# Attention scores in plain float32 on sixteen 32x32 array tiles, with K turned on the host

## The reference

```
scores = einsum('bsgrd,btgd->bgrst', xq, xk) / sqrt(32)     # 8 groups g, 4 heads r, 32 numbers d
scores = scores + mask                                      # s: 32 rows, t: 257 tokens
probs  = softmax(scores);  out = einsum('bgrst,btgd->bsgrd', probs, xv)
```

## Time and profile before

| | |
|---|---|
| median of 2 runs | 1293.69 us (1291.55 to 1295.84) |
| span of the profiled execution | 1290.8 us, 42154 instructions |
| PE busy | 1238.7 us, 96% |
| PEld busy | 1074.4 us, 83% |
| ACT busy | 1122.5 us, 87% |
| DVE busy | 1046.6 us, 81% |
| POOL busy | 824.7 us, 64% |
| DMA | 166.45 MB, 270940 packets, 195433 of them under 512 B |
| chain of work that ended last | PE 86%, DVE 4%, SP's queue 3% |

### The profile page before, as it was taken

One profiled execution on the slowest core, in us unless ns is written; L12 is line 12 of the kernel. 1 busy time (PEld: TensorE's weight loads), 2 busy tenths in 40 slices (PEclk: granted clock), 3 DMA queues, 4 the chain that ended last, 5 costly groups with the idle time before them and its releaser, 6 DMA issues.

```text
span 1290.8 us, 42154 instructions
## 1 busy us (share of the span) xinstructions
PE 1238.7 (96%) x13676; PEld 1074.4 (83%) x13676; DVE 1046.6 (81%) x3552; ACT 1122.5 (87%) x3337; POOL 824.7 (64%) x1259
## 2 busy tenths in 40 slices
PE   4679999999999999999999999999999999999997
PEld 3558888888888888888888888888888888888886
DVE  7978788888888888888888888878888888888753
ACT  5999898998999899899998989998999999898851
POOL 5376666776666677666667766667776666676420
PEclk9899999999999999999999999999999999999999
DMA  8754445554545545454454555445445445554210
GB/s 230 172 133 127 113 128 138 133 143 121 138 127 129 138 123 145 130 140 120 135 138 122 145 131 134 125 121 144 129 123 153 130 116 138 129 140 123 60 59 33
DMA packets 270940, 166.45 MB, mean 129 GB/s; under 512 B 195433, under 2 KB 253298, under 8 KB 270722
## 3 DMA queue, kind: packets, MB, share of 16 engines
q1 hardware_dynamic: 270722, 163.74, 47.5%
HBM read 128.50 MB, written 34.08 MB: 126 GB/s over the span
## 4 chain that ended last, share of the span: by engine, by line
PE 86%; DVE 4%; SPq 3%; issue 2%; DMA 2%; ACT 2%; POOL 1%; DVEq 0%; ACTq 0%; POOLq 0%
PE ps_p L566 25%; PE ps_p L637 16%; PE ps_p L652 15%; PE ps_p L665 14%; PE ps_p L598 9%; PE ps_s L578 8%; SPq L385 2%; DVE ms L1401 1%; DMA dn<-den 1%; ACT pr L853 1%; DVE x L1257 0%; DMA qx<-turn_q 0%; SPq L373 0%; DMA vl<-in_ctx 0%; PE ps_p L524 0%
## 5 line engine op out<-in xcount | busy, mean ns | idle before, releaser
L853 ACT ACTIVATE pr<-ms,negmax 128x256 f32<-128x256 f32 x1024 | 514.7, 505 | 3.8 <-DVE negmax L1401 3.7
L1401 DVE CUSTOM_DVE_ANT_0 ms<-ps_s,neg_mask,last 128x256 f32<-128x256 f32 x1024 | 457.5, 471 | 34.9 <-PE ps_s L578 30.2
L785 ACT ACTIVATE pts<-ps_p 128x512 f32<-128x512 f32 x512 | 295.9, 592 | 48.2 <-PE ps_p L566 44.2
L566 PE MATMUL ps_p<-ident,pr 128*128 128x128 f32 x2048 | 304.8, 277 | 12.0 <-ACT pr L853 4.9
L566 PEld LDWEIGHTS ps_p<-ident,pr 128*128 128x128 f32 x2048 | 238.2, 141 | 49.2 <-issue 16.0
L853 ACT ACTIVATION_READ_ACCUMULATOR pr<-ms,negmax 128x1 f32 x1024 | 200.6, 196 | 0.0
L1075 POOL TENSOR_TENSOR kt<-kr,kt 128x512 fp32r<-128x512 f32 x128 | 165.1, 1290 | 27.9 <-ACT kt L785 27.3
L652 PE MATMUL ps_p<-wa_hi,ut_hi 128*128 128x288 f32 x512 | 177.7, 347 | 1.4 <-DVE ut_lo L1217 1.4
L652 PE MATMUL ps_p<-wa_lo,ut_hi 128*128 128x288 f32 x512 | 151.0, 295 | 0.0
L652 PE MATMUL ps_p<-wa_hi,ut_lo 128*128 128x288 f32 x512 | 150.7, 294 | 0.0
L1117 POOL TENSOR_TENSOR lastp<-lastp 128x256 f32<-128x256 f32 (+4 forms) x320 | 128.7, 402 | 22.6
(11 more groups left out here) (140 smaller groups left out, 2709.6 us busy)
## 6 DMA issues: line engine op xcount, KB each, us to landing
cx<-in_ctx SPq DMA_DIRECT2D x128, 256.0 KB, 3.0
kx<-in_ctx SPq DMA_DIRECT2D x512, 64.0 KB, 2.4
xq<-in_x SPq DMA_DIRECT2D x32, 512.0 KB, 4.2
turn_q<-xq SPq DMA_DIRECT2D x32, 512.0 KB, 3.7
qx<-turn_q SPq DMA_DIRECT2D x128, 128.0 KB, 3.0
xr<-in_x SPq DMA_DIRECT2D x32, 512.0 KB, 4.4
out_x<-tmp SPq DMA_DIRECT2D x32, 512.0 KB, 5.2
dn<-den SPq DMA_DIRECT2D x512, 2.0 KB, 2.0
```

What stands on the lines that cost most here:

```text
L566: mm = pe.transpose(into[:, j * P:(j + 1) * P], source, ident[:, :])
L785: return act.activation(out, in_, ACT.Copy, scale=scale)
L853: act.activation(pr[:, b % 2, g, :], ms[:, n % MS, :], ACT.Exp, bias=negmax[:, n % MS:n % MS + 1], scale=-1.0, accum_out=den[:, b, g:g + 1 ...
L1401: dve.tensor_tensor_reduce(ms[:, n % MS, :], ps_s[:, g % GPH, g // GPH * SW:(g // GPH + 1) * SW], neg_mask[:, 0:SW], 1.0, last[:, it % 2, ...
```

## The change

The host gives K turned (`io["keys"]`: 128 partitions of quad and d, then half and token). SP loads a batch with one DMA of 2 KB rows into `kt`, which is now plain float32. `k_turn`, `k_high`, `k_low`, `q_high` and `q_low` are gone; `q_turn` writes straight into `qr`, which has two buffers. `scores` multiplies plain float32, and takes the four r apart: each matmul has 32 rows, 32 columns of weights and 256 moving columns and stands in one of the 16 places of 32x32, in 2 halves x 4 r x 4 quads = 32 matmuls for each batch. A matmul of plain float32 is again load, pass, load, pass.

```diff
             def load_keys(tile, b):
 
-                if at(tile, BPT, b - 1) > 0:
-                    sp.wait_ge(kr_done, at(tile, BPT, b - 1))
-                turned = context[tile * BPT + b:tile * BPT + b + 1, 0:2 * P, :].rearrange(
-                    "o (c t) (q e) -> (o t) c q e", t=HEAD_DIM, q=GPH)
-                for quad in range(GPH):
-                    sp.dma_start(kx[HEAD_DIM * quad:HEAD_DIM * (quad + 1), b % 2, :, :, :].rearrange("p c h d -> p c (h d)"),
-                                 turned[:, :, quad, :]).then_inc(kx_loaded[b], 16)
+                if tile > 0:
+                    sp.wait_ge(s_done, at(tile - 1, BPT * GPH, GPH * (b + 1)))
+                sp.dma_start(kt[:, b, :, :].rearrange("p h t -> p (h t)"),
+                             io["keys"][tile * BPT + b:tile * BPT + b + 1, :, :].rearrange("o p c -> (o p) c")).then_inc(kx_loaded[b], 16)
...
             def scores(it, b):
-                pe.wait_ge(kl_done, at(it, BPT, b + 1))
+                pe.wait_ge(kx_loaded[b], at(it, 16, 16))
                 if b == 0:
-                    pe.wait_ge(ql_done, at(it, 2, 2))
+                    pe.wait_ge(qr_done, at(it, 2, 2))
                 pe.wait_ge(ms_done, at(it, STEPS, GROUPS * b))
                 for h in range(HALVES):
-                    for j, (q_part, k_part) in enumerate(((0, 0), (0, 1), (1, 0))):
+                    for r in range(REP):
                         for quad in range(GPH):
                             rs = slice(HEAD_DIM * quad, HEAD_DIM * (quad + 1))
-                            mm = pe.matmul(ps_s[:, quad, h * SW:(h + 1) * SW], qs[rs, it % 2, q_part, b, h, :, :].rearrange("p r s -> p (r s)"),
-                                           kt[rs, b, k_part, h, :], start=(j == 0), stop=(j == 2), skip_group_check=True)
-                            if j == 2 and h == HALVES - 1:
+                            mm = pe.matmul(ps_s[SEQ * r:SEQ * (r + 1), quad, h * SW:(h + 1) * SW], qr[rs, it % 2, h, b, r, :],
+                                           kt[rs, b, h, :], start=True, stop=True, skip_group_check=True)
+                            if r == REP - 1 and h == HALVES - 1:
                                 mm.then_inc(s_done, 1)
...
-            def k_turn(tile, b):
-                dve.wait_ge(kx_loaded[b], at(tile, 64, 64))
-                dve.wait_ge(kl_done, at(tile, BPT, b))
-                dve.transpose(kr[:, :, :].rearrange("p h (c t) -> p c h t", t=HEAD_DIM),
-                              kx[:, b % 2, :, :, :]).then_inc(kr_done, 1)
-
             def q_turn(tile, h):
                 dve.wait_ge(q_moved, at(tile, 64, 64))
-                dve.wait_ge(ql_done, at(tile, 2, h))
-                dve.transpose(qr[:].rearrange("p b r s -> p b (r s)"),
+                if at(tile, BPT * GPH, -BPT * GPH) > 0:
+                    dve.wait_ge(s_done, at(tile, BPT * GPH, -BPT * GPH))
+                dve.transpose(qr[:, tile % 2, h, :, :, :].rearrange("p b r s -> p b (r s)"),
                               qx[:, :, h, :, :].rearrange("p b r d -> p b (r d)")).then_inc(qr_done, 1)
```

More of the change, by code:

```diff
@@ L689, in iteration @@
                 if on(it - 1):
-                    attend(it - 1, 4); attend(it - 1, 5)
+                    attend(it - 1, 4)
+                    attend(it - 1, 5)
                 if on(it - 2):
@@ L700, in iteration @@
                 if on(it - 1):
-                    attend(it - 1, 6); attend(it - 1, 7)
+                    attend(it - 1, 6)
+                    attend(it - 1, 7)
                 pair_chunk(it, 2)
@@ L717, in iteration @@
                 pair_chunk(it, 5)
-                attend(it, 0); attend(it, 1)
+                attend(it, 0)
+                attend(it, 1)
                 pair_chunk(it, 6)
@@ L742, in iteration @@
                     z_chunk(it - 1, 0, 1 - odd)
-                attend(it, 2); attend(it, 3)
+                attend(it, 2)
+                attend(it, 3)
                 if on(it - 1):
@@ L752, in _ @@
[L752 to L760, removed]
+            weight_chunk(2, 1); pair_chunk(0, 1); scores(0, 1); weight_chunk(3, 0); pair_chunk(0, 2); pair_chunk(0, 3)
+            weight_chunk(3, 1); pair_chunk(0, 4); weight_chunk(4, 0); scores(0, 2); weight_chunk(4, 1); attend(0, 0)
@@ new lines, in _ @@
+            attend(0, 1); pair_chunk(0, 5); pair_chunk(0, 6); weight_chunk(5, 0); weight_chunk(5, 1); pair_chunk(0, 7)
+            dft_product(); pair_chunk(0, 8); scores(0, 3); weight_chunk(6, 0); pair_chunk(0, 9); kernel_rows()
+            pair_chunk(0, 10); pair_chunk(0, 11); attend(0, 2); attend(0, 3); weight_chunk(6, 1); scores(1, 0)
+            weight_chunk(7, 0); pair_chunk(0, 12); pair_chunk(0, 13); pair_chunk(0, 14); strip_part(0)
+            pair_chunk(0, 15); attend(0, 4); attend(0, 5); scores(1, 1); pair_chunk(1, 0); strip_part(1)
@@ new lines, in _ @@
+            pair_chunk(1, 1); attend(0, 6); attend(0, 7); strip_part(2); pair_chunk(1, 2); pair_chunk(1, 3)
+            out_chunk(0, 0); weight_chunk(7, 1); scores(1, 2); out_chunk(0, 1); pair_chunk(1, 4); attend(1, 0)
+            attend(1, 1); pair_chunk(1, 5); pair_chunk(1, 6); pair_chunk(1, 7); pair_chunk(1, 8); attend(1, 2)
+            attend(1, 3); u_chunk(0, 0); scores(1, 3); u_chunk(0, 1); pair_chunk(1, 9); convolve(0, 0, 0, 4)
+            convolve(0, 1, 0, 2); pair_chunk(1, 10); convolve(0, 1, 2, 8); z_chunk(0, 0, 0); z_chunk(0, 1, 0)
@@ L936, in iteration @@
                 exp(it, 2)
-                k_high(it, 3)
                 exp(it, 3)
@@ L988, in iteration @@
                     u_high(it - 1, 1)
-                if on(it + 1):
-                    q_high(it + 1, 0)
                 exp(it, 21)
-                if on(it + 1):
-                    k_high(it + 1, 1)
                 pair_copy(it, 9)
@@ L1002, in iteration @@
                 exp(it, 28)
-                if on(it + 1):
-                    q_high(it + 1, 1)
                 exp(it, 29)
-                if on(it + 1):
-                    k_high(it + 1, 2)
                 if on(it - 1):
@@ L1161, in iteration @@
             def iteration(it, odd):
-                k_low(it, 1)
-                q_low(it, 1)
                 if on(it - 1):
                     last_shift(it - 1, 3)
-                k_low(it, 2)
                 if on(it - 2):
@@ L1171, in iteration @@
                 last_shift(it, 0)
-                k_low(it, 3)
                 if on(it - 1):
@@ L1200, in _ @@
[L1200 to L1203 removed]
+            row_scale(0, 0); last_product(0, 0); last_sum(0, 0); last_mask(0, 0); last_product(0, 1); last_sum(0, 1)
@@ L1540, in iteration @@
                 maximum(it, 3)
-                k_turn(it, 3)
                 maximum(it, 4)
@@ L1658, in _ @@
+            maximum(1, 31); second_residual(0, 1, 0); q_stats(3, 1); z_low(0, 0); z_low(0, 1)
             for it in range(HEAD, TAIL):
```

249 lines of the change are left out of this document (99 added, 150 removed).

## The result

The changed kernel took 1356.48 us (two runs, 1353.58 and 1359.38) where the kernel before took 1293.69. The ratio is 1.049, with a 95% interval from 1.0464 to 1.0517: slower by about 63 us. The forecast was 1329 us in a range of 1300 to 1385, so the sign and the range held and the size was 27 us short.

A forecast was written before the change was run, and what follows sets the result against it. PE's own work was taken to bound the kernel from 128 us on. 1290.8 + 45 (scores) - 8 (ahead of 98 us) = 1327.8, less 1 for scores in idle time, plus 2 to the median: 1329 us, range 1300 to 1385.

The forecast's parts named there:

- What bounds the kernel: From 128 us on PE's own work sets the time; relief of other engines is worth at most 2.0 us.
- The scores: PE's scores were to take 1.27 us a batch, 0.35 more than before, 45 us over 128 batches.
- The lower bound's parts: Scores with all sixteen places at once: passes of 0.216 us, 7 ns steps, together 1.09 us, 0.17 more than before.
- the reading of the queue: PE's queue holds 64 to some 74 instructions, freed in program order as they end; chance 0.52.
- 0.62 + 0.03 + 14 x 0.007 = 0.75: Start in us of the last waiting matmul in the scores' second half, after room at 0.62, with 7 ns steps.
- all sixteen at once: Rival for the scores: queue frees instructions earlier than their recorded end, 0.17 us more a batch, 1307 us; chance 0.20.
- Passes in strict order: Rival for the scores: each second pass waits for its first, 7.1 us a batch, about 2085 us; chance 0.03.
- faster: Rival for the scores: a 32x32 place takes a column at 0.42 ns, 0.25 us less a batch, 1251 us; chance 0.02.
- A shorter look ahead: Rival for the scores: passes overtake over fewer than 58 instructions, 0.64 us more a batch or above, 1367 to 1417; chance 0.20.
- Ahead of 98 us: Start of the kernel: relief of the other engines ends a DVE hold of up to 8.8 us; 8 us gained, bounds 0 and 13.
- 8 + 1: Gain in us ahead of 98 us, plus 1 for scores of tiles 0 and 1 that lie in idle time.
- A: Queue theory for computing the second half twice: 64 instructions, filled at 4.2 ns each, 2.0 us a batch, span near 1428 us.

The follow-up runs named there:

- hosted: Kernel before with only K turned on the host, one transfer a batch, no DVE turns of K, SP waiting for POOL's low part: 1305.72 us, ratio 1.0084.
- relief: Changed kernel with scores as three equal bfloat16 products on four row places, not the reference's scores: 1275.38 us, ratio 0.9864.
- hosted3: Kernel before with only K turned on the host, its loads going round three buffers with the wait three batches back: 1288.97 us, ratio 0.9981.
- triple16: Changed kernel with one-pass bfloat16 products on sixteen places, each done three times, 192 instructions a batch: 1.091 us a batch.
- rows4: Changed kernel with plain float32 scores on four row places of 32x128 instead of sixteen of 32x32: 1311.19 us, ratio 1.0134.
- half: Changed kernel with only the first half of each batch's scores from the second tile on: 0.645 us a batch, span 1259.9 us.
- single16: Changed kernel with one bfloat16 pass a matmul on sixteen places, 64 instructions a batch: 0.381 us a batch, span 1241.3 us.
- quadfirst: Changed kernel with the quad loop outside the r loop, turning round the order of places: 1.425 us a batch, span 1359.4 us.
- after2: Changed kernel with K's buffer doubled by tile, so loads of K wait for scores two tiles back: span 1351.3 us.
- three: Changed kernel with the second half of scores computed twice, 192 plain float32 instructions a batch: 2.056 us a batch, span 1451.3 us.

## Why the prediction was right in sign and short in size

**What bounds the kernel.** Right. But for hosted, with its wait on SP, the span of each kernel that computes all of the scores in full follows from PE's work on them: 0.911, 1.050, 1.077 and 1.426 us a batch go with spans of 1285.0 to 1290.8, 1303.7, 1310.5 and 1351.3 to 1359.4. The spread of 6 to 8 us at equal work comes in the main from the first stretch. ACT and DVE came to 76% and 71%, where 75 and 72 were said. What the others were relieved of was worth 0 to 2 us after 128 us, as priced; relief and hosted3 show it with PE's work held down or the same.

**The scores.** Right in mechanism, one term mis-sized. The lower bound's parts held: a pass of 256 columns at 0.216 us, passes of different places that start while older ones wait, sixteen starts in 0.10 us, the next set 0.24 us on. So did the reading of the queue: the second half began at 0.650 us where 0.65 was said, and a half alone took 0.645. The room is the low end of what I read, 64: in triple16 the 66th instruction (the 33rd pass) starts at 0.313, 0.026 us behind the recorded end of the second (0.287), and in the changed kernel the instructions behind the 68th start from 0.646 on, 0.032 us behind the recorded end of the fourth (0.614). The term that failed is "0.62 + 0.03 + 14 x 0.007 = 0.75". The 16.7 ns step stands in its place, and 14 of them are 0.23 us. I took the 7 ns step from `attend`, whose instructions, most likely, stood ready in the queue when they ran. In the changed kernel the second half's instructions only come in as room is made, and they come at 4.2 ns each, 16.7 ns a matmul. The last first pass started at 0.883 instead of 0.75, and after its two passes and the emptying this is 1.43 instead of 1.27 us. The other 0.16 us a batch is 21 us of the 27 by which the forecast was short.

Split by cause: rows4 has plain float32 in place of three products and costs 1.077 - 0.911 = 0.166 us a batch, some 21 us; the step from four places to sixteen costs 1.426 - 1.077 = 0.349, some 45 us. Without the queue the change would most likely have been near the rival *all sixteen at once*, which half and single16 show to be true for a group of instructions that has room, and only for such a one. For packed tiles the Trainium skill ("TensorE: Matmul & The Clock Gate", section "Measured speedup vs the span model") gives some 4 ns for each further tile. Within the first 64 instructions the trace is near it: 3.3 ns for a matmul of one pass in single16, 6.7 ns for one of two passes here. Behind them it is not: the step is 16.7 ns here and 8.3 ns in triple16, and a batch takes 0.34 us more than my 1.09 us for all at once.

*Passes in strict order* is refuted by the sixteen first passes in 0.10 us, *faster* by the 0.24 us to the second set. *A shorter look ahead* (0.64 us and more over before) did not happen, though 0.515 lies closer to it than to my 0.35.

**Ahead of 98 us.** Here the reading was wrong. I forecast 8 us, chiefly from a hold of DVE of 8.8 us between two maxima. The maximum of tile 1 moved from 67.56 only to 67.27 us. The row that I did not read is that stretch of the kernel before, with its busy times (columns as in the earlier trace rows):

```profile
58.76:67.56 8.80, 7.82 (x108) 6.35 (x107) 7.64 (x30) 7.82 (x25) 2.90 (x4) 0.81 0.19 35
```

DVE was busy for 7.64 of the 8.80 us, and PE and ACT for 7.82. The trace has nine further maxima of tile 0 and two `wb_lo` splits in that gap. Nor could the maximum of tile 1 have come much sooner: tile 1's first scores ran from 66.27 to 67.19 us, on PE, behind work of tile 0. In the changed kernel they start at 65.72 and the maximum waits for them, not for POOL (start us, us, what):

```profile
65.72 1.52 PE ps_s L566 x61
```

They end at 67.24, 0.03 us ahead of the maximum. The chain leaves out what does not end last; its 5.54 us of "issue" was POOL's, and I read a step of the chain as idle time of DVE. With POOL's `q_low` and `k_low` gone, DVE had the same work to do but for one `k_turn` of 0.7 us. What did shrink is PE's idle time by 5.2 us in all, 2.0 of them the waits after 128 us. What the other 3 are was not shown. It may be cover, the longer scores of the first tiles growing into gaps where PE would have waited anyway: relief, with shorter scores, kept 50.5 us of idle time, and the changed kernel has 46.9. But quadfirst and after2, with scores as long as the changed kernel's, have 53.1 and 49.3, so single runs differ by more than those 3 us. The forecast had 8 + 1 for this, and the profiled run has 5.2.

**The sum again.** 66.3 us of scores where I had 45, 5.2 given back where I had 9, and 4.7 us from the profiled run to the median where I had 2: short by 21.3, 3.8 and 2.7 us, together 27.8.

What sets the pace ahead of 98 us was not settled. Not the low parts of q and K (relief), and in the changed kernel not SP's wait for the scores (after2). hosted showed that one wait on SP makes it some 12 us longer (11.4 us from tile 0's first scores to tile 4's, 161.8 against 150.4). ACT's 9.4 us were not tested by themselves.

## What to carry to other kernels

More and smaller places on the array cost instructions, and TensorE's instructions have a pace of their own: count what a group needs (places x loads and passes) against the queue, and if it does not fit, use fewer and wider places. Here 64 ran at the streams' pace and 128 did not. A step between instructions that is read where they stood ready does not hold where they have to be brought in. A gap in the chain that ended last is not idle time until the engine's own busy time over the same stretch says so; and a wait on the queue that issues the loads must be judged by what stands behind it, and by the clock that PE is granted behind it, as hosted showed.

## What the runs showed that I had not expected

The queue has a pace for filling, 4.2 ns an instruction on TensorE, in plain float32 and bfloat16 alike, against 1.7 ns (6.7 / 4 and 3.3 / 2) for those that stand in it.

With 192 instructions for each batch PE at times had nothing to start at all. triple16's span was 68 us above that of the kernel before, where its scores, by their median, explain 23. In 31 of its 128 batches the scores took over 1.19 us and up to 3.3; with them the scores add up to 170.2 us against 118.7, which explains 51.5 of the 68. The chain that ended last in one of them:

```profile
521.37 1.07 PE ps_s L568 x93
522.44 1.70 issue
524.14 0.29 PE ps_s L568 x2
```

PE waited 1.70 us ahead of the batch's last two matmuls, for nothing that the profile shows. PE's longest waits of this sort from 200 to 1200 us, in triple16 and then in three:

```profile
PE ps_s L568 <- issue: 19.2, 17, 2.0
PE ps_p L555 <- issue: 4.7, 4, 1.6
```

```profile
PE ps_s L566 <- issue: 6.3, 8, 1.5
```

In three the batches add up to 281.9 us, 18.7 more than 128 medians, and this is most of the 23 us by which its span was above A's. The queue of instruction loads moved 3.01 MB in triple16 and in three, 2.49 in the changed kernel and 1.84 before. That the engine waited for the next piece of its program is the likely reading, and it was argued, not shown. The changed kernel has no such wait: its longest batch after 128 us took 1.426 us.

A batch of as many passes on as many places took 0.790 us in relief (bfloat16) and 0.911 in the kernel before (fp32r). The weight loads of 32x128 took 91 to 95 ns there and 181 to 187 here. In the records 0.093 of the 0.121 us lie ahead of the second set of passes, which starts at 0.128 us where it started at 0.221, its loads at 0.011 where they started at 0.106; the later sets follow every 0.113 us instead of every 0.118. So most of it is the weights at the start of a batch. When I expected 0.91 us for relief I had taken such loads for hidden, since PE never waited in the rows.
